# Moving the last pass over the tokens beside the last nine expert blocks of a two-layer kernel

## The chip, the core and the metric

The kernel runs on one core of a Trainium2 chip. The metric is the device time of one execution in microseconds; lower is better. All tensors are float32.

## What is computed

Two layers run over 4096 tokens (`B*S`) of 256 features. Each layer normalises `x`, computes a sequence-mixing term `s` and a mixture-of-experts term, and adds `s * silu(experts)` to `x`. The change touches only the end of layer 1 and a few things that it needs earlier:

```python
xn = _layernorm(x)
s = _L1_attn_ref(xn, ...)     # spectra of three projections, unit magnitude, product, cumsum over tokens, inverse
# mixture of 8 experts, two for every token
gate_scores = softmax(xn @ Wg + bg)
topk_scores, topk_idx = top_k(gate_scores, 2)
topk_scores = topk_scores / (sum(topk_scores) + 1e-08)
for e in range(8):
    h = gelu(xn @ W1[e] + b1[e])              # 256 -> 1024
    y = h @ W2[e] + b2[e]                     # 1024 -> 256
    output = output + y * combine_w[..., e:e + 1]
x = x + s * silu(output)
```

## The kernel before

**Order.** Everything is placed by hand. `schedule0` writes the plan of layer 0, `schedule1` that of layer 1: a list of items such as `("w1", n)`. Each engine walks the same list and carries out those items that concern it, in that order, so the list sets the order on every engine and on the DMA queues of SP (SyncE) and POOL (GpSimd). An item that waits holds everything behind it on its engine.

**Layer 1, attention.** The 4096 tokens are 16 chunks of 256. For a chunk, TensorE makes the spectra, ScalarE squares them (`squares`, L1963), POOL adds real and imaginary squares (L2074), ScalarE takes the root (`magnitudes`, L1970), which needs another activation table than GELU does (`ACT_TABLE_LOAD`), and VectorE does the rest of the chunk (`bind`, some 16 instructions). The spectra of the first eight chunks are made before the expert blocks; chunks 0 to 2 get their roots there too.

**Layer 1, routing.** Each token has two results, one for each of its two experts. Rows are sorted by expert into 71 tiles of 128 rows. VectorE finds which token stands in which row by comparisons (`rows_of`, 8 groups of `hot_tile`, L1626, and `hot_row`, L1629, multiplied by TensorE at L1143). Its answer is `token_of` (which row to fetch) and `result_of` (where the result goes, 0 to 8191).

**Layer 1, experts.** The tiles make 39 blocks: 32 pair blocks of two tiles (numbers 0 to 31) and then 7 single blocks of one tile. Block `n` runs as: POOL fetches its rows by an indirect DMA per tile (`xg`, L2086); TensorE turns them (L1165) and multiplies by `W1` (L1179) in eight pieces through three banks; ScalarE applies GELU to each piece (L1996); TensorE multiplies by `W2` (L1189); VectorE adds the bias (L1734); POOL scatters each tile into `result1` by an indirect DMA (L2097). SP loads each block's weights (L2239, 2180 KB) three blocks ahead. Chunk `n + 1` of the attention stands beside block `n`.

**The end.** When all results are in DRAM, item `last` goes over the tokens in eight quarters `q` of 512 tokens: SP loads both results of a quarter (`both`, L2251, 1 MB), ScalarE weighs the first (L2006), VectorE adds the weighed second (L1742), ScalarE applies SiLU (L2015), VectorE multiplies by `s` (L1753) and adds `x` (L1755), SP stores (L2254). `x` and `s` of all quarters (`xs`) were loaded at block 19 by one item (16 DMAs of 512 KB).

```python
# L2013: ScalarE, one quarter of the last pass
first = both[q][:, 0, :, :]
w.wait_ge(mixed1, q + 1)
e.activation(first, first, ACT.Silu).then_inc(gated1, 1)
```

## Time and profile before

| | us |
|---|---|
| median of 3 runs | 1188.36 (1184.89 to 1188.45) |
| the profiled execution's own time | 1180.72 |
| its span, first to last instruction | 1178.6 |
| PE busy | 1035.9 (88%) |
| DVE busy | 650.8 (55%) |
| ACT busy | 526.5 (45%) |
| POOL busy | 368.0 (31%) |

PE is TensorE's matrix products, PEld its weight loads, DVE VectorE, ACT ScalarE, POOL GpSimd, SP SyncE. An execution's own time is 2.1 us longer than its span. Busy shares are means over the whole span; what a piece of work costs has to be read in the stage where it stands. The page's busy line of PE by slices of 29.5 us reads 9 (90% or more) nearly everywhere from 118 us on, is lower around 420 to 560 us, and falls to 4 and then 0 in the last two slices.

### The profile page before, as it was taken

How to read it: one execution, taken by the hardware profiler on the slowest of the kernel's cores; microseconds unless marked ns; L12 is line 12 of the kernel's file. 1: busy time of each engine (PE TensorE's matmuls, PEld its weight loads, DVE VectorE, ACT ScalarE, POOL GpSimd, SP SyncE). 2: the span in 40 equal slices, each digit the busy share in tenths (PEclk: the TensorE clock that was granted, in tenths of full speed). 3: DMA queues.
4: the chain of work that ended last, by engine and by line, in shares of the span. 5: the costliest groups of instructions: out<-in, count | busy, mean ns of one | idle time of the engine just before them, and what ended most of it. 6: DMA issues, size and time to landing. Idle time of an engine off the chain costs nothing.

```text
span 1178.6 us, 16522 instructions
## 1 busy us (share of the span) xinstructions
PE 1035.9 (88%) x6152; PEld 889.6 (75%) x6152; DVE 650.8 (55%) x1379; ACT 526.5 (45%) x1079; POOL 368.0 (31%) x352
## 2 busy tenths in 40 slices
PE   4468999999999947887999999999999999999940
PEld 3347788888888835676878888888888888889930
DVE  7578776776777758686998566575300000000028
ACT  4324655554554456614354544454233323333445
POOL 1046545445445420003244232323222222222200
PEclk9779999999999988878999999999999999999975
DMA  9914234433444354344376334253555975555848
GB/s 299 266 55 145 80 107 123 145 105 111 131 131 120 121 181 161 118 191 163 122 267 250 137 139 170 108 198 134 193 203 198 360 303 195 204 201 192 328 144 283
DMA packets 100911, 208.65 MB, mean 177 GB/s; under 512 B 9850, under 2 KB 86150, under 8 KB 95840
## 3 DMA queue, kind: packets, MB, share of 16 engines
q1 hardware_dynamic: 89264, 176.27, 43.1%
q0 software_dynamic: 11568, 31.34, 8.0%
q8 instruction: 49, 0.80, 0.3%
q14 instruction: 30, 0.25, 0.1%
HBM read 159.86 MB, written 49.75 MB: 178 GB/s over the span
## 4 chain that ended last, share of the span: by engine, by line
PE 70%; DVE 15%; DMA 5%; ACT 4%; SPq 3%; issue 2%; POOL 0%; POOLq 0%; DVEq 0%; ACTq 0%
PE PS L1189 18%; PE PS L1179 17%; PE PS L1078 6%; PE PS L913 6%; PE PS L963 4%; PE PS L1017 3%; PE PS L972 2%; PE PS L1044 2%; PE PS L1088 2%; PE PS L1030 2%; PE PS L1055 2%; DVE hot_tile L1626 1%; SPq L2213 1%; SPq L2214 1%; DVE stats L1211 1%
## 5 line engine op out<-in xcount | busy, mean ns | idle before, releaser
L1996 ACT ACTIVATE hT<-PS,WE 128x256 f32<-128x256 f32 (+1 forms) x312 | 140.5, 455 | 281.6 <-PE PS L1179 278.2
L1179 PE MATMUL PS<-xgT,WE 128*128 128x256 f32 (+1 forms) x1248 | 256.2, 363 | 6.4 <-ACT hT L1996 4.1
L1189 PE MATMUL PS<-WE,hT 128*128 128x256 f32 x1136 | 251.6, 379 | 0.0
L1179 PEld LDWEIGHTS PS<-xgT,WE 128*128 128x128 f32 x1248 | 219.8, 191 | 35.9 <-ACT hT L1996 6.9
L1189 PEld LDWEIGHTS PS<-WE,hT 128*128 128x128 f32 x1136 | 213.4, 190 | 27.7
L1734 DVE TENSOR_TENSOR y<-PS,WE 128x512 f32<-128x512 f32 (+1 forms) x39 | 25.1, 643 | 353.0 <-PE PS L1189 353.0
L2097 POOL DMA_INDIRECT result<-y,result_of x71 | 71.7, 1009 | 285.0 <-DVE y L1734 271.2
L2074 POOL TENSOR_TENSOR MAG<-SQ 128x768 f32<-128x768 f32 x16 | 29.6, 1851 | 220.6 <-ACT SQ L1963 220.6
L913 PE MATMUL PS<-XT,Wf 128*128 128x256 f32 x384 | 96.1, 409 | 0.0
L913 PEld LDWEIGHTS PS<-XT,Wf 128*128 128x128 f32 x384 | 78.0, 208 | 11.4
L2086 POOL DMA_INDIRECT xg<-xn_dram,token_of x71 | 73.0, 1029 | 29.9 <-issue 21.5
L2055 POOL TENSOR_TENSOR prob<-prob,row_sum 128x512 f32<-128x512 f32 x56 | 58.6, 1047 | 59.9 <-DVE row_sum L1384 59.5
L1078 PE MATMUL PS<-rowsT,wgu 128*128 128x160 f32 x512 | 75.6, 301 | 0.0
L1078 PEld LDWEIGHTS PS<-rowsT,wgu 128*128 128x128 f32 x512 | 71.9, 190 | 2.3 <-issue 1.4
L2048 POOL TENSOR_TENSOR sc<-sc,sc_max 128x512 f32<-128x512 f32 x56 | 58.6, 1047 | 42.4 <-DVE sc_max L1372 42.1
L963 PE MATMUL PS<-XT,qkv_w 128*128 128x256 f32 x256 | 67.1, 409 | 0.0
L902 PE MATMUL PS<-const,XN 128*128 128x128 f32 x128 | 25.4, 331 | 45.4 <-DVE XN L1227 40.8
L1382 DVE TENSOR_REDUCE row_sum<-prob 128x8 f32<-128x512 f32 x64 | 43.6, 681 | 26.6 <-ACT prob L1864 25.8
L902 PEld LDWEIGHTS PS<-const,XN 128*128 128x128 f32 x128 | 17.2, 163 | 54.4 <-DVE XN L1227 23.3
L963 PEld LDWEIGHTS PS<-XT,qkv_w 128*128 128x128 f32 x256 | 49.7, 205 | 8.5 <-issue 0.4
L2066 POOL DMA_INDIRECT mixed_dram<-y,row_token x40 | 39.8, 996 | 47.3 <-DVE y L1438 42.9
L2039 POOL DMA_INDIRECT table<-XN,slot_put x32 | 32.0, 1001 | 66.3 <-DVE slot_put L1315 49.6
(240 smaller groups left out, 1600.8 us busy)
## 6 DMA issues: line engine op xcount, KB each, us to landing
WE<-in_experts SPq DMA_DIRECT2D x39, 2180.0 KB, 9.0
wgu<-in_w_gate SPq DMA_DIRECT2D x32, 256.0 KB, 2.8
wgu<-in_w_up SPq DMA_DIRECT2D x32, 256.0 KB, 3.2
wdn<-in_w_down SPq DMA_DIRECT2D x32, 256.0 KB, 3.5
both<-result SPq DMA_DIRECT2D x16, 512.0 KB, 8.8
table<-zeros POOLq DMA_DIRECT2D x1, 5160.0 KB, 32.7
rows<-table SPq DMA_DIRECT2D x32, 129.0 KB
X<-in_x SPq DMA_DIRECT2D x8, 512.0 KB, 8.7
```

The lines of the kernel that those rows point to most:

```text
L902: m = e.transpose(out_v[:, k, j * P:(j + 1) * P], XN[:, 2 * pair + j, k * P:(k + 1) * P], ident)
L913: m = e.matmul(PS[:, u.bank, part * CH:(part + 1) * CH], Wf[:, n, k, part * P:(part + 1) * P], XT1[:, ch, k, :], start=k == 0, stop=k == K ...
L963: m = e.matmul(PS[:, u.bank, c * UT:(c + 1) * UT], qkv_w[:, k, col:col + P], XT0[:, unit, k, :], start=k == 0, stop=k == KD - 1)
L1078: m = e.matmul(PS[:, u.bank + f, n * CAP:(n + 1) * CAP], wgu0[:, ex % 2, n, k, f * P:(f + 1) * P], rowsT[:, grp % 2, k, j * CAP:(j + 1) * ...
L1179: m = e.matmul(PS[:, FIRST_H_BANK + nth % HR, 0:rows], W1[n % WR][:, k, c * P:(c + 1) * P], xgT[:, n % 2, k, 0:rows], start=k == 0, stop=k ...
L1189: m = e.matmul(PS[:, u.bank, j * D:(j + 1) * D], hT[:, n % 2, c, j * P:(j + 1) * P], W2[n % WR][:, c, :], start=c == 0, stop=c == KF - 1)
L1382: e.tensor_reduce(row_sum[:, s % RR, :], prob[:, s % PR0, :, :], AX.X, ALU.add).then_inc(row_sum_done, 1)
L1996: e.activation(hT[:, n % 2, c, 0:rows], PS[:, FIRST_H_BANK + (KF * n + c) % HR, 0:rows], ACT.Gelu_apprx_tanh, bias=b1[n % WR][:, c:c + 1], ...
L2048: e.tensor_tensor(by_head, by_head, sc_max[:, s % SR, :].unsqueeze(2).to_broadcast([P, PAIRS, WIN]), ALU.subtract).then_inc(sc_sub_done, 1)
L2055: e.tensor_tensor(prob[:, s % PR0, :, :], prob[:, s % PR0, :, :], row_sum[:, s % RR, :].unsqueeze(2).to_broadcast([P, PAIRS, WIN]), ALU.mu ...
L2086: e.indirect_dma_start(out=xg[:, n % XR, j, :], out_offset=None, in_=xn_dram, in_offset=bass.IndirectOffsetOnAxis(ap=token_of[:, tile:tile ...
L2097: e.indirect_dma_start(out=result1, out_offset=bass.IndirectOffsetOnAxis(ap=result_of[:, tile:tile + 1], axis=0), in_=y1[:, n % YR, j, :], ...
```

## The change

The last pass is taken apart and put beside the last nine blocks, and the blocks are put in another order for it.

- **Blocks.** The single blocks stand among the pair blocks (positions 16, 18, ... 28), so that the last nine blocks (`EARLY` = 30 to `LAST` = 38) are pairs.
- **Two result tables.** The results of blocks 0 to 29 are scattered twice, into `result1` and `other1`; those of blocks 30 to 37 into `other1` alone; those of block 38 nowhere. Both tables are filled with zeros beforehand, by 32 DMAs of 512 KB in layer 0.
- **Quarters beside the blocks.** Item `last`'s eight quarters run in blocks 31 to 36 (1, 1, 1, 1, 2, 2 quarters). They read `result1`; a token with a result in a late block gets a value there that is overwritten later. SiLU is written as a tanh, which needs no other table than GELU: `0.5 z (1 + tanh(z/2))`.
- **Late rows.** For each of the 18 late tiles, POOL fetches `x`, `s` and the two weights of its tokens (`late_rows`, 2064-byte rows of a new table `late_dram`), and the token's other result from `other1` (`late_other`); VectorE and ScalarE finish those rows (`late_sum`, `late_gate`, `late_rest`), and POOL scatters them to the output after all quarters are stored (`late_put`). Where both results of a token are late, only the later row is put (`put_of`).
- **Last block.** Its `W2` product is made in two halves (`w2_last`), each finished by itself.
- **Root sums.** VectorE adds the squares of chunks 0 to 2 (`first_sum`) in place of POOL. The roots of chunks 3 and 4 stand at block 2 instead of block 1.
- **Small.** `xg` is fetched three blocks ahead instead of two; `xs` has five buffers, filled one a block from block 17; the weights are saved as 16-byte pieces in `late_dram` (4096 of them).

```diff
-SLOT_TILES = [2] * PAIR_SLOTS + [1] * SINGLE_SLOTS
+LATE, FIRST_SINGLE = 9, 16
+BLOCKS = [(2, 2 * n) for n in range(PAIR_SLOTS)]
+for n in range(SINGLE_SLOTS):
+    BLOCKS.insert(FIRST_SINGLE + 2 * n, (1, 2 * PAIR_SLOTS + n))
...
+XSR, BR, OR = 5, 3, 3
+XS_AT, LATE_ROWS_AT = CHUNKS + 1, CHUNKS + 1
+MIXED_AT = [[], [0], [1], [2], [3], [4, 5], [6, 7]]
+LAGGED = EARLY + len(MIXED_AT) - 1
+PUT_FIRST, PUT_SECOND = 4, 6
...
         if i == 4:
-            for ch in range(ROOTS_AHEAD):
-                add("squares", ch)
-    for ch in range(ROOTS_AHEAD):
-        add("magnitudes", ch)
+            for ch in range(2):
+                add("first_sum", ch)
+            add("squares", 2)
+            for ch in range(2):
+                add("magnitudes", ch)
+    add("first_sum", 2)
+    add("magnitudes", 2)
...
+        if n == 2:
+            add("magnitudes", ch)
+            add("magnitudes", ch + 1)
...
+        mixed = MIXED_AT[n - EARLY] if EARLY <= n <= LAGGED else ()
+        if EARLY + 2 <= n <= LAGGED + 1:
+            add("late_gate", n - 2)
+            add("late_rest", n - 2)
+        if n > LAGGED:
+            add("late_sum", n - 1)
+            add("late_gate", n - 1)
+            add("late_rest", n - 1)
+        for q in mixed:
+            add("weigh", q)
+            add("mix", q)
+        for q in mixed:
+            add("gate1", q)
+        if n < LAST:
+            add("w2", n)
+        else:
+            for j in range(2):
+                add("w2_last", j)
+        for q in mixed:
+            add("store", q)
+        if EARLY < n <= LAGGED:
+            add("late_sum", n - 1)
...
+        if n == LAST - 1:
+            for m in range(PUT_FIRST, PUT_SECOND):
+                add("late_put", EARLY + m)
+        if EARLY <= n + 1 < NSLOT:
+            add("late_other", n + 1)
+        if n == LAST - 2:
+            for m in range(PUT_FIRST):
+                add("late_put", EARLY + m)
+        if n == LAST - 1:
+            for m in range(EARLY + PUT_SECOND, LAST):
+                add("late_put", m)
...
+        def late_rest(n, some):
...
+            e.scalar_tensor_tensor(out=z, in0=gate, scalar=1.0, in1=z, op0=ALU.add, op1=ALU.mult).then_inc(
...
+            e.scalar_tensor_tensor(out=z, in0=z, scalar=0.5, in1=fin[:, tiles, D:2 * D], op0=ALU.mult, op1=ALU.mult).then_inc(
...
+            m = e.tensor_tensor(fin[:, tiles, 0:D], fin[:, tiles, 0:D], z, ALU.add)
...
+        def late_put(n, j):
+            tile = 2 * (n - EARLY) + j
+            w.wait_ge(late_ready, tile + 1 if n == LAST else tile - j + 2)
+            wait_stored(w, QUARTERS)
+            w.wait_ge(selected, 2)
+            e.indirect_dma_start(
+                out=out, out_offset=bass.IndirectOffsetOnAxis(ap=put_of[:, tile:tile + 1], axis=0), in_=fin[:, tile, 0:D],
...
+            elif what == "late_other":
+                wait_results1(w, n)
...
+            elif what == "store":
+                q, = at
+                w.wait_ge(out_ready, q + 1)
+                e.dma_start(out_view[:, 4 * q:4 * q + 4, :], xs[q % XSR][:, 0, :, :]).then_inc(stored[q % XSR], 16)
+                if q + BR < QUARTERS:
+                    load_both(q + BR)
+                if q and q - 1 + XSR < QUARTERS:
+                    load_xs(q - 1 + XSR)
```

On POOL, at the end of the program, these rows stood before (`result` is the scatter of a tile, `xg` the fetch):

```order
L2097 DMA result<-y_163,result_of 8192x256
L2086 DMA xg<-xn_dram,token_of 128x256
L2097 DMA result<-y_163,result_of 8192x256
L2086 DMA xg<-xn_dram,token_of 128x256
L2097 DMA result<-y_163,result_of 8192x256 x3
L2258 UNCONDITIONAL_BRANCH
```

and these stand there now, from block 35 on (`other<-y` is the scatter of a block's results, `other_174<-other` and its like the fetch of the other results for the next block, `out<-fin` the late rows to the output):

```order
L2328 DMA other<-y_176,result_of 8192x256 x2
L2351 DMA other_174<-other,other_of 128x256 x2
L2328 DMA other<-y_176,result_of 8192x256 x2
L2351 DMA other_178<-other,other_of 128x256 x2
L2294 DMA out<-fin,put_of 4096x256 x8
L2328 DMA other<-y_176,result_of 8192x256 x2
L2294 DMA out<-fin,put_of 4096x256 x4
L2351 DMA other_188<-other,other_of 128x256 x2
L2294 DMA out<-fin,put_of 4096x256 x6
```

Eight output scatters (those of blocks 30 to 33) stand between block 36's fetch and block 37's scatter, and four more (blocks 34 and 35) ahead of block 38's fetch.

On ACT, in the first expert blocks, stood before (`SQ` the squares of a chunk, `MAG` the roots, `hT` the eight GELUs of a block, from block 0 on):

```order
L1996 ACTIVATE hT<-PS,WE 128x256 x8
L1983 ACTIVATE xgT<-PS 128x512
L1963 ACTIVATE SQ<-Z 128x512 x3
L1996 ACTIVATE hT<-PS,WE 128x256 x8
L1983 ACTIVATE xgT<-PS 128x512
L1963 ACTIVATE SQ<-Z 128x512 x3
L1970 ACT_TABLE_LOAD
L1970 ACTIVATE MAG<-MAG 128x768 x2
L1996 ACT_TABLE_LOAD
L1996 ACTIVATE hT<-PS,WE 128x256 x8
```

and now:

```order
L2215 ACTIVATE hT<-PS,WE 128x256 x8
L2202 ACTIVATE xgT<-PS 128x512
L2182 ACTIVATE SQ<-Z 128x512 x3
L2215 ACTIVATE hT<-PS,WE 128x256 x8
L2202 ACTIVATE xgT<-PS 128x512
L2182 ACTIVATE SQ<-Z 128x512 x3
L2215 ACTIVATE hT<-PS,WE 128x256 x8
L2202 ACTIVATE xgT<-PS 128x512
L2189 ACT_TABLE_LOAD
L2189 ACTIVATE MAG<-MAG 128x768 x2
L2182 ACTIVATE SQ<-Z 128x512 x3
L2215 ACT_TABLE_LOAD
```

The pair of table loads has moved from ahead of block 2's GELUs to behind them, ahead of a chunk's squares.

On DVE, in the last groups of the routing, stood before:

```order
L1626 TENSOR_SCALAR hot_tile<-const,tile_f 128x71 x8
L1629 TENSOR_TENSOR hot_row<-const,in_tile 128x1024
L1636 COPY row_v<-PS 128x71
L1638 TENSOR_SCALAR row_empty<-row_v 128x71
L1639 TENSOR_SCALAR row_v<-row_v 128x71
```

and now, from group 4 on:

```order
L1772 TENSOR_SCALAR hot_tile<-const,tile_f 128x71 x8
L1775 TENSOR_TENSOR hot_row<-const,in_tile 128x1024
L1782 TENSOR_TENSOR MAG<-SQ 128x768 x2
L1772 TENSOR_SCALAR hot_tile<-const,tile_f 128x71 x8
L1775 TENSOR_TENSOR hot_row<-const,in_tile 128x1024
L1772 TENSOR_SCALAR hot_tile<-const,tile_f 128x71 x8
L1775 TENSOR_TENSOR hot_row<-const,in_tile 128x1024
L1772 TENSOR_SCALAR hot_tile<-const,tile_f 128x71 x8
L1775 TENSOR_TENSOR hot_row<-const,in_tile 128x1024
L1782 TENSOR_TENSOR MAG<-SQ 128x768
L1786 COPY row_v<-PS 128x71
```

The three sums (`MAG<-SQ`) have come to DVE, two behind group 4 and one behind group 7; POOL has none of them any more.

## Rows read from the trace of the kernel before

**Rows 1.** Stages: length, busy (count) of PE, PEld, DVE, ACT, POOL; clock, DMA, GB/s

```profile
500.00:560.00 60.00, 47.49 (x236) 42.47 (x236) 46.16 (x142) 20.52 (x40) 11.48 (x9) 0.77 0.46 180
...
860.00:920.00 60.00, 60.00 (x288) 52.83 (x287) 2.77 (x4) 17.41 (x36) 16.25 (x16) 1.00 0.55 205
920.00:960.00 40.00, 38.32 (x184) 33.46 (x183) 2.08 (x3) 12.86 (x27) 12.19 (x12) 1.00 1.06 385
```

**Rows 2.** Waits of PE over 560 to 1132 us: total, times, longest us

```profile
PE PS L1179 <- ACT hT L1996: 4.1, 7, 2.9
PE PS L1179 <- DMA WE<-in_experts: 1.7, 1, 1.7
PE PS L1165 <- DMA xg<-xn_dram,token_of: 0.7, 1, 0.7
```

**Rows 3.** Timeline of the end: start us, us, instructions [idle before <-releaser]

```profile
1128.28 3.62 PE L1189 MATMUL PS<-WE,hT 128*128 128x256 f32 x16
...
1131.93 0.42 DVE L1734 TENSOR_TENSOR y<-PS,WE 128x256 f32<-128x256 f32 x1 [6.60 <-PE PS L1189]
1133.13 0.97 POOL L2097 DMA_INDIRECT result<-y,result_of  x1 [6.05 <-DVE y L1734]
...
1140.82 1.71 ACT L2006 ACTIVATE both<-both,weight 128x256 f32<-128x256 f32 x4 [10.46 <-DMA both<-result]
...
1145.44 1.04 ACT L2015 ACTIVATE both<-both 128x1024 f32<-128x1024 f32 x1
...
1168.80 1.66 DVE L1742 SCALAR_TENSOR_TENSOR both<-both,weight 128x256 f32<-128x256 f32 x4
...
1174.03 1.22 DVE L1755 TENSOR_TENSOR xs<-xs,both 128x1024 f32<-128x1024 f32 x1
```

**Rows 4.** Chain that ended last, the result's scatter: start us, us, what

```profile
1133.13 2.08 DMA result<-y,result_of
```

**Rows 5.** Timeline of POOL in a stretch of plain pair blocks

```profile
866.32 1.01 POOL L2097 DMA_INDIRECT result<-y,result_of  x1 [10.17 <-DVE y L1734]
867.64 0.99 POOL L2097 DMA_INDIRECT result<-y,result_of  x1 [0.30 <-issue]
...
880.59 1.01 POOL L2097 DMA_INDIRECT result<-y,result_of  x1 [9.30 <-DVE y L1734]
```

**Rows 6.** Groups over 860 to 920 us: count, busy us, mean ns

```profile
L1996 ACT ACTIVATE hT<-PS,WE 128x256 f32<-128x256 f32 x32 | 15.2, 474 | 39.6 <-PE PS L1179 39.6
...
L1734 DVE TENSOR_TENSOR y<-PS,WE 128x512 f32<-128x512 f32 x4 | 2.8, 692 | 53.4 <-PE PS L1189 53.4
...
L1983 ACT ACTIVATE xgT<-PS 128x512 f32<-128x512 f32 x4 | 2.4, 597 | 0.0
```

**Rows 7.** DMA issues of the page: count, KB each, median us to landing

```profile
WE<-in_experts SPq DMA_DIRECT2D x39, 2180.0 KB, 9.0
...
both<-result SPq DMA_DIRECT2D x16, 512.0 KB, 8.8
...
out<-xs SPq DMA_DIRECT2D x8, 512.0 KB, 4.9
```

**Rows 8.** Timeline of the routing's last groups

```profile
531.92 1.90 DVE L1626 TENSOR_SCALAR hot_tile<-const,tile_f 128x71 f32<-128x71 f32 x8 [2.78 <-PE PS L1143]
...
537.81 6.53 DVE L1626 TENSOR_SCALAR hot_tile<-const,tile_f 128x71 f32<-128x71 f32 x8
537.96 5.42 POOL L2074 TENSOR_TENSOR MAG<-SQ 128x768 f32<-128x768 f32 x3 [113.64 <-ACT SQ L1963]
```

**Rows 9.** Timeline of expert blocks 1 and 2

```profile
590.19 1.28 ACT L1970 ACT_TABLE_LOAD   x1
...
591.48 1.58 ACT L1970 ACTIVATE MAG<-MAG 128x768 f32<-128x768 f32 x2
...
608.55 0.69 DVE L1734 TENSOR_TENSOR y<-PS,WE 128x512 f32<-128x512 f32 x1 [0.77 <-PE PS L1189]
...
610.34 1.21 POOL L2097 DMA_INDIRECT result<-y,result_of  x1 [3.97 <-issue]
```

More of the change, by code:

```diff
@@ L27 @@
 PAIR_SLOTS, SINGLE_SLOTS = T * TOPK // (2 * P), E1 - 1
[L28 to L29 removed]
+LATE, FIRST_SINGLE = 9, 16
+BLOCKS = [(2, 2 * n) for n in range(PAIR_SLOTS)]
+for n in range(SINGLE_SLOTS):
+    BLOCKS.insert(FIRST_SINGLE + 2 * n, (1, 2 * PAIR_SLOTS + n))
+SLOT_TILES, SLOT_AT = [tiles for tiles, _ in BLOCKS], [at for _, at in BLOCKS]
 NSLOT = len(SLOT_TILES)
+EARLY, LAST = NSLOT - LATE, NSLOT - 1
+LATE_AT, LATE_TILES = SLOT_AT[EARLY], 2 * LATE
+assert all(BLOCKS[EARLY + n] == (2, LATE_AT + 2 * n) for n in range(LATE))
 TILES1 = sum(SLOT_TILES)
@@ L473, in add @@
             banks.take(item, 5)
+        elif what == "w2_last":
+            banks.take(item, (5, 7)[at[0]])
     def spectra(ch):
@@ L499, in schedule1 @@
             add("owners")
+        if i == 1:
+            add("squares", 0)
+            add("squares", 1)
         if i in (2, 4):
@@ L864, in wait_attn1_end @@
         w.wait_ge(summed, 2 * CHUNKS)
-    def wait_experts_read(w):
-        for n in (NSLOT - 2, NSLOT - 1):
-            u = use["w2", n]
-            w.wait_ge(full[u.bank], u.filled)
     def score_of(PS, s):
@@ L1190, in tensor @@
                                      W2[n % WR][:, c, :], start=c == 0, stop=c == KF - 1)
+                m.then_inc(full[u.bank], 1)
+            elif what == "w2_last":
+                j, = at
+                u = use["w2_last", j]
+                fill_from(u)
+                for c in range(KF):
+                    w.wait_ge(gelu_done, KF * LAST + c + 1)
+                    m = e.matmul(PS[:, u.bank, 0:D], hT[:, LAST % 2, c, j * P:(j + 1) * P], W2[LAST % WR][:, c, :],
+                                 start=c == 0, stop=c == KF - 1)
                 m.then_inc(full[u.bank], 1)
@@ L1632, in vector @@
                                 ALU.is_equal).then_inc(hot_row_ready, 1)
+            elif what == "first_sum":
+                ch, = at
+                w.wait_ge(squared, ch + 1)
+                e.tensor_tensor(MAG[:, ch, :, :], SQ[:, ch % 2, :, 0, :], SQ[:, ch % 2, :, 1, :], ALU.add).then_inc(mag_ready, 1)
             elif what == "rows_found":
@@ L1732, in vector @@
                 else:
[L1733 removed]
+                    w.wait_ge(y_out[n % YR], y1_landed(n % YR, n))
                 e.tensor_tensor(y1[:, n % YR, 0:tiles, :], PS[:, u.bank, 0:tiles * D].rearrange("p (j d) -> p j d", d=D),
                                 b2[n % WR].unsqueeze(1).to_broadcast([P, tiles, D]), ALU.add).then_inc(free[u.bank], 1)
[L1736 to L1755 removed]
@@ L2126, in load_gate_up, with zero_results @@
                 e.dma_start(wgu0[:, ex % 2, n, :, :], a[name][ex].rearrange("(k p) n -> p k n", p=P)).then_inc(gu_in[ex % 2], 16)
+        def zero_results(ex):
+            nth = ZERO_AT.index(ex)
+            first = ZERO_ROWS * nth
+            w.wait_ge(filled, 4)
+            for results in (result1, other1):
+                e.dma_start(results[first:first + ZERO_ROWS, :].rearrange("(r p) d -> p r d", p=P),
+                            zeros[:, 0:D].unsqueeze(1).to_broadcast([P, ZERO_ROWS // P, D])).then_inc(results_zeroed, 16)
         def load_down(ex):
```

381 lines of the change are left out of this document (279 added, 102 removed).

## The prediction, written before the changed kernel ran

> **What bounds the kernel now.** I read the stages first: from the end of the routing on, TensorE has no gap to speak of. In a stretch of plain pair blocks it is busy for 60.00 of 60 us at the full clock, while VectorE has 2.77 us of work, ScalarE 17.41 and POOL 16.25 [rows 1]. The waits of TensorE over the whole of the blocks come next: 4.1 us for GELU (one of 2.9), 1.7 for weights, 0.7 for rows [rows 2]. So work of the other engines is free beside the blocks as long as nothing waits for it, and TensorE's time there can hardly shrink. Third, the timeline of the end: TensorE's last product ends at 1128.28 + 3.62 = 1131.9, the span at 1178.6. For 46.7 us TensorE has nothing to do: bias and scatter (landed at 1135.2), a load, and eight quarters at some 4.1 us of VectorE each (1.66 and twice 1.22), its last addition starting at 1174.03 [rows 3, 4]. Last, the stretch of 500 to 560 us, where TensorE works 47.49 of 60 us at a granted 0.77 and waits for VectorE's routing [rows 1, 8].
>
> **The end, new.** The eight quarters go beside blocks 31 to 36. A pair block's period is 880.59 - 866.32 = 14.27 us [rows 5]. I follow the last blocks from t = 0, the end of block 35's products.
>
> VectorE first: bias 0.7 [rows 6], then three operations of 1024 columns for each of quarters 4 and 5. The trace has no scalar_tensor_tensor of that width; four of 256 took 1.66, a tensor_tensor of 1024 took 1.22 [rows 3]; I take 1.22, the row of the same width. That is 3.7 a quarter, ending at 8.1. Block 34's sums (four operations of 256 columns, 0.42 each) end at 9.8. ScalarE has by then finished block 36's GELUs and the copy (7.5 + 0.6, at 8.1 [rows 6]); tanh of block 34 to 10.7, weighing of quarters 6 and 7 (1.71 each [rows 3]) to 14.1. VectorE does the rest of block 34 (three of 512 columns at 0.69 [rows 6]) to 12.8 and the two mixes (1.66 each) to 16.2; ScalarE's last tanh (1.04 [rows 3]) ends at 17.2. Block 37's GELUs stand behind it. TensorE starts block 37 at 14.27, fills three banks (of eight pieces in half a period, 0.9 each) in 2.7 and wants the first GELU's answer by 17.0; it comes at 17.2 + 0.47: a stall of 0.7 us. The single-quarter blocks have room.
>
> VectorE's bias of block 36 ends at 16.9, its six operations at 24.2; the last quarter is stored 4.9 later [rows 7], at 29.1. Only then do POOL's output scatters start. One indirect DMA takes POOL 1.32 from start to start [rows 5]. Eight of them: 39.7. Block 37's two scatters, which have been ready since about 31: 42.3. Four more output scatters: 47.6. The two fetches for block 38: the second starts at 48.9 and, with 2.08 from start to landing in a quiet stretch [rows 4], lands at 51.0. TensorE ends at 14.27 + 0.7 + 14.27 + 13.8 = 43.0 (the last block turns no rows for a next one, an estimate of 0.5 less). So VectorE's last work waits for the queue, not for TensorE. From 51.0: scaling two tiles 0.8; for each half bias 0.42, sum 0.41, tanh 0.43, three operations of 0.42 and some 0.2 of hand-overs, 2.7; twice is 5.4, at 57.2; from there to the landing of the last scatter 1135.2 - 1132.35 = 2.9 [rows 3, 4], at 60.1. The tail is 17.1 us in place of 46.7: **-29.6**, and **+0.7** for the stall.
>
> **Other terms.** (a) In the routing's last group, eight comparisons that take 1.90 take 6.53 beside POOL's three sums of 5.42 [rows 8]. They go to VectorE: 768 columns, between 0.69 and 1.22 each, two of them in the 2.78 us in which VectorE waits for TensorE behind group 4 [rows 8], one behind group 7, while TensorE multiplies that group. So 4.6 us go; two small copies of the changed `owners` add 0.3: **-4.3**. (b) TensorE's wait of 2.9 in block 2 goes with the table loads ahead of its GELUs [rows 2, 9]. They now stand where TensorE has block 2's second product, 7 us, against 6.5 of ScalarE: a copy of 0.6, two loads of 1.28, two roots of 1.58 together, three squares of 512 columns at the copy's 0.6 [rows 6, 9]. VectorE gets chunk 3's roots some 4 us later; in block 2 its bias waited only 0.77 for TensorE [rows 9], but block 3's second product comes 8 us behind it and is what needs it: **-2.9**, at worst 0. (c) The wait of 1.7 for weights stands where 16 loads of 512 KB go out at once, at 385 GB/s [rows 1, 2]; they are now spread: **-1.7**. The 0.7 for rows in the single blocks goes too: there is one single block in 21.5 us and three blocks of advance: **-0.7**. (d) The zeros are 32 x 0.5 MB in layer 0, where I found no load that TensorE waits for, the 4096 pieces of 16 bytes stand ahead of the spectra's saves, and blocks 0 to 29 scatter 53 tiles twice. POOL has 53 x 1.32 = 70 us more in some 440, and it idles for 10 us in each plain block [rows 5]; nothing waits for the second copies. No row prices the 16-byte pieces; they can't gain anything, and the nearest row, 512 KB of output in 4.9 [rows 7], is my upper bound; I take **+1.5** for all of (d).
>
> Sum: -29.6 + 0.7 - 4.3 - 2.9 - 1.7 - 0.7 + 1.5 = -37.0. Against the profiled execution's own 1180.7 that is 1143.7. The runs shown have a median of 1188.4, 7.6 above it; the difference belongs to both kernels alike, so 1151.4, and I forecast **1151**. A change of under 0.3% (3.6 us) can't be told from none.
>
> **Rivals.**
>
> *The queue doesn't hold the end.* If stores land sooner and block 38's rows are fetched before TensorE is done, the tail is one half's 2.7 and the landing of 2.9, 5.6: 11.5 better, 1140. It needs block 38's fetch some 12 us sooner: a store that lands as fast as the scatter's 2.08 in place of 4.9 [rows 4, 7], less work of VectorE than I count, or scatters closer together than 1.32. For it, the DMAs are quiet by then; against it, VectorE has some 15 us of work in a block with two quarters, so that quarter 7 can't come much sooner. 12%.
>
> *Crowded transfers, and ScalarE in order.* A late block moves 2.2 MB of weights, 1.05 of results in, 0.52 of output, 0.79 of rows and, three times, 1.05 of `x` and `s`: 5.6 MB in 14.27 us is 395 GB/s, above the 385 of the busiest stretch, in which TensorE did wait [rows 1]. Each quarter's weighing stands ahead of a block's GELUs; where its load comes late, TensorE stops. Against it: loads are issued two blocks before use, except quarter 7's (one block, some 6 us of spare against 8.8 to landing [rows 7]). With 2.5 us in each of six blocks: +15, 1166. 19%. By the Trainium skill (DMA: Bandwidth & Descriptors, Specifications) HBM gives a core about 358 GB/s; the 385 of the trace is above that, one core running alone here. At 358 the three blocks would fall behind by 1.5 us each, an estimate that would make this rival likelier.
>
> *POOL slowed by VectorE.* Beside a busy VectorE one scatter took 1.21 instead of 1.01 [rows 5, 9]. With 0.2 more on each of the 16 operations between the last store and block 38's fetch: +3.2, 1155. 9%. The Trainium skill (DMA: Bandwidth & Descriptors, SWDGE vs HWDGE vs iDMA) says why it may be so: POOL writes its descriptors to on-chip memory that VectorE's two-port modes lock it out of. The trace agrees by those 0.2 us.
>
> *The gains ahead don't come.* If chunk 3's later roots or the pieces of 16 bytes give back (a) and (b): +7, 1158. 9%.
>
> *Slower.* SP's queue becomes the clock: a block's weight load now stands behind the store of a quarter, which waits for VectorE, which waits for ScalarE, which waits for a load that itself stands behind weights. If that ring closes, each of blocks 31 to 38 lasts longer than 14.27; from 4.6 us a block on (37 / 8) the change loses. At 6 us a block it would be 1151 + 48 = 1199. Against it: three weight buffers give two blocks, 28 us, against 9.0 to landing [rows 7]. 4%. Something between this and the crowded case, within 0.3% of before: 2%.
>
> **Numbers.** The forecast has 45% with 1145 to 1157, the rivals 12, 19, 9, 9, 4 and 2. For 8 in 10 I take in the first and most of the crowded case: 1139 to 1167. Faster 0.94, same 0.02, slower 0.04.
>
> **What would show it.** Right: TensorE's last product some 15 to 18 us ahead of the end; POOL back to back with output scatters, and a wait of VectorE's for a fetch of `other` in that tail; `hot_tile` without a 6.5 us group; no wait over 1 us for GELU in block 2; blocks 30 to 38 at 14.3 us. Wrong: periods above 15 us there (crowding: TensorE waiting for `hT` behind `both`), a tail of under 8 (the queue), or a stretch of 500 to 560 us in which TensorE is no busier than 47.49.

## The result, and the profile after

The first set of runs gives 1192.10 us as the median of 7 for the changed kernel against 1187.19 for the kernel before, in the same set: a ratio of 1.0048, 95% interval 1.0025 to 1.0072. That is a loss of half a per cent, small but outside the noise. I had forecast 1151 us, and the time lies outside my range. The profiled execution took 1186.6 us, its span is 1184.8.

The same kernel was then run again, on other chips, as the baseline of the experiments. The comparison comes out in two ways, and each whole set lies on one side:

| set | chip | before, median (n) | changed, median (n) | ratio (95%) |
|---|---|---|---|---|
| 1 | not known | 1187.19 (7) | 1192.10 (7) | 1.0048 (1.0025 to 1.0072) |
| 3 | index 0 | 1180.38 (11) | 1157.91 (4) | 0.9803 (0.9771 to 0.9836) |
| 4 | index 8 | 1179.19 (11) | 1156.61 (7) | 0.9814 (0.9796 to 0.9831) |
| 5 | index 13 | 1180.34 (7) | 1159.57 (4) | 0.9840 (0.9796 to 0.9885) |
| 6 | index 14 | 1186.19 (25) | 1190.56 (10) | 1.0047 (1.0018 to 1.0076) |

Sets 2 (chip index 9, before 1178.26) and 7 (index 0 again, before 1185.02) held other kernels. I call 1, 6 and 7 the late sets, for what their traces show, and 2 to 5 the clear sets. The trace of before shown ahead of the prediction is a clear one: its 1180.72 us lie under all seven timed runs of its own set (1182.30 to 1188.45), and only 12 of its 8480 DMA semaphore updates are missing (a clear trace of the changed kernel lacks none to 14 of 10,688).

First the stages of the late trace, in the stretches of [rows 1] (length, busy time of PE, PEld, DVE, ACT, POOL, then clock, DMA share, GB/s), with 960 to 1030 added:

```profile
500.00:560.00 60.00, 51.15 (x250) 45.44 (x248) 47.89 (x157) 22.38 (x45) 6.07 (x6) 0.80 0.49 162
860.00:920.00 60.00, 54.95 (x273) 46.67 (x271) 2.66 (x5) 17.11 (x41) 27.08 (x28) 0.94 0.79 287
920.00:960.00 40.00, 34.04 (x176) 28.76 (x177) 1.81 (x3) 10.80 (x27) 15.44 (x16) 1.00 0.81 303
960.00:1030.00 70.00, 64.22 (x341) 55.25 (x340) 6.03 (x33) 22.30 (x53) 38.19 (x38) 1.00 0.73 269
```

From the trace of the same kernel in set 4:

```profile
860.00:920.00 60.00, 60.00 (x333) 54.23 (x333) 3.35 (x6) 21.04 (x50) 32.38 (x33) 1.00 0.91 341
920.00:960.00 40.00, 40.00 (x224) 36.14 (x223) 2.23 (x4) 13.37 (x34) 21.45 (x22) 1.00 0.84 313
960.00:1030.00 70.00, 70.00 (x352) 62.14 (x351) 13.17 (x44) 26.68 (x58) 36.84 (x37) 1.00 0.80 287
```

TensorE loses 16.8 of 170 us in the late trace, by its busy time, and nothing in the clear one, whose DMA moves more in the same time. The stalls cost clock as well. After a stretch in which TensorE worked 2.21 of 5 us the granted clock falls to 0.50, its lower level of 1.2 GHz, from 894.1 to 900.9 us:

```profile
890.00:895.00 5.00, 2.21 (x8) 1.31 (x8) 0.00 (x0) 0.47 (x1) 3.72 (x4) 0.91 1.12 416
895.00:900.00 5.00, 4.41 (x11) 3.52 (x12) 0.00 (x0) 2.38 (x6) 0.00 (x0) 0.50 0.94 384
```

TensorE is busy for 5.3 us of that, so I estimate 2.7 us lost to the clock. PE's waits from 560 us on, late (set 1) and then clear (set 4):

```profile
PE PS L1281 <- issue: 13.6, 13, 2.4
PE PS L1281 <- ACT hT L2215: 9.3, 14, 3.4
PE PS L1267 <- DMA xg<-xn_dram,token_of: 2.5, 1, 2.5
```

```profile
PE PS L1281 <- ACT hT L2215: 7.7, 8, 3.4
```

L1281 is the `W1` product. "issue" means that the view knows no releaser; the timeline of pair block 19 in the late trace shows one (start us, us, instructions, idle before and releaser):

```profile
885.02 2.75 PE L1281 MATMUL PS<-xgT,WE 128*128 128x256 f32 x12
887.05 1.00 POOL L2315 DMA_INDIRECT xg<-xn_dram,token_of  x1 [0.30 <-issue]
888.03 0.47 ACT L2215 ACTIVATE hT<-PS,WE 128x256 f32<-128x256 f32 x1 [5.33 <-PE PS L1281]
888.56 1.13 PE L1281 MATMUL PS<-xgT,WE 128*128 128x256 f32 x4 [0.79 <-issue]
891.53 0.47 ACT L2215 ACTIVATE hT<-PS,WE 128x256 f32<-128x256 f32 x1 [1.63 <-PE PS L1281]
892.06 1.13 PE L1281 MATMUL PS<-xgT,WE 128*128 128x256 f32 x4 [0.98 <-issue]
893.62 1.01 POOL L2315 DMA_INDIRECT xg<-xn_dram,token_of  x1 [0.31 <-issue]
895.07 0.47 ACT L2215 ACTIVATE hT<-PS,WE 128x256 f32<-128x256 f32 x1 [3.06 <-remote]
895.59 3.78 PE L1281 MATMUL PS<-xgT,WE 128*128 128x256 f32 x8 [2.40 <-issue]
```

TensorE runs three pieces through its three banks and stops; ScalarE stands idle and starts the first GELUs 2 to 5.4 us after their pieces ended (a piece ends by 886.0, its GELU starts at 888.03; the fourth piece, of 888.56 to 889.69, gets its GELU at 895.07); 0.05 us behind each GELU TensorE goes on. So neither engine is slow and no data are missing; I read this as TensorE's completion signals arriving late, and TensorE's own DRAIN in the later traces (below) bears it out. They cost time in the pair blocks 19, 21, 23, 25 and 29, each behind a single block, while POOL issues 12 indirect DMAs in a row (13 in the last one). Here the row is from 879.2 to 894.6 us, and the signals are on time from 895.1 on. The length of the row does not decide alone: block 27 has a row of 11 over 14.1 us beside its product, GELUs there are 1.6 us late at most, and TensorE loses nothing; and in this trace the row of 20 at the end (1145.9 to 1172.8 us) delays none of TensorE's signals that the trace shows. What is different there is not known. In the clear trace the same row stands beside the same product:

```profile
893.55 7.07 PE L1281 MATMUL PS<-xgT,WE 128*128 128x256 f32 x32
894.69 0.47 ACT L2215 ACTIVATE hT<-PS,WE 128x256 f32<-128x256 f32 x1 [3.81 <-PE PS L1281]
895.47 0.47 ACT L2215 ACTIVATE hT<-PS,WE 128x256 f32<-128x256 f32 x1 [0.31 <-PE PS L1281]
895.62 1.00 POOL L2315 DMA_INDIRECT xg<-xn_dram,token_of  x1 [0.30 <-issue]
```

The page of the late trace has a second mark: DMAs without a landing time. Late, then clear:

```profile
WE<-in_experts SPq DMA_DIRECT2D x39, 2180.0 KB
```

```profile
WE<-in_experts SPq DMA_DIRECT2D x39, 2180.0 KB, 10.3
```

Each DMA gives 16 semaphore updates, 10,688 in this kernel. The late traces record 7991 (set 1) and 7884 (set 6) of them, the clear ones at least 10,674. The Trainium skill (NOTIFIC — the notification-queue block, Overflow: three behaviours, one of which stalls the engine) says that a full notification queue either loses records or stalls the engine that makes them. Lost records and late signals stand together in all five late traces (one in set 1, three in set 6, one in set 7). That does not make the queue the cause: no run here shows the queue itself, the losses are also where nothing is late (34 to 36 updates of 128 in each of blocks 6 to 12 of the first late trace), and a run of set 5 loses some without a late signal. The timed runs are late as well.

The end, in the late trace (DVE and POOL rows chosen; TensorE's last product ends at 1161.06):

```profile
1153.99 7.07 PE L1300 MATMUL PS<-WE,hT 128*128 128x256 f32 x32
1163.80 0.98 POOL L2294 DMA_INDIRECT out<-fin,put_of  x1 [0.30 <-issue]
1166.43 1.02 POOL L2351 DMA_INDIRECT other<-other,other_of  x1 [0.30 <-issue]
1169.37 0.80 DVE L1601 TENSOR_SCALAR other<-other,other_weight 128x256 f32<-128x256 f32 x2 [11.86 <-DMA other<-other,other_of]
1175.10 0.42 DVE L1615 TENSOR_TENSOR fin<-fin,other 128x256 f32<-128x256 f32 x1
1176.32 0.97 POOL L2294 DMA_INDIRECT out<-fin,put_of  x1 [1.71 <-DVE fin L1615]
```

The tail is 1184.8 - 1161.1 = 23.7 us in place of 46.7 [rows 3]; in the clear traces it is 23.8, 21.7 and 29.2. VectorE waits for the fetch behind POOL's puts, as forecast. Behind the last put's landing stands POOL's own last instruction, a DRAIN, from 1178.81 to 1184.60 us. In the trace of before POOL's DRAIN is at 1132.91, 5.36 us long, and nobody waits for it.

In the four late traces of sets 6 and 7 the tail has late signals too, and longer ones. In `combined` (set 6) TensorE's last product ends at 1144.80, the other results are scaled by 1149.22, and VectorE gets to the last block's bias at 1156.65, 2.4 us behind POOL's row:

```profile
1142.70 2.10 PE L1297 MATMUL PS<-WE,hT 128*128 128x256 f32 x9
1153.24 0.98 POOL L2291 DMA_INDIRECT out<-fin,put_of  x1 [0.30 <-issue]
1156.65 0.42 DVE L1939 TENSOR_TENSOR y<-PS,WE 128x256 f32<-128x256 f32 x1 [7.43 <-remote]
```

TensorE's own DRAIN ends 11.8 to 14.8 us behind its last product in these four, and within 0.1 us of it in the other traces. VectorE so waits 3.9 us in `after_fifth` and `end_on_sp`, 7.4 and 5.9 in `combined` and `combined_again`; no edit was aimed at this.

Routing in the clear trace of set 4 (DVE; the comparisons of the last groups, then the third root sum), which answers to [rows 8]:

```profile
528.22 1.90 DVE L1772 TENSOR_SCALAR hot_tile<-const,tile_f 128x71 f32<-128x71 f32 x8 [0.83 <-PE PS L1245]
534.12 1.89 DVE L1772 TENSOR_SCALAR hot_tile<-const,tile_f 128x71 f32<-128x71 f32 x8
537.06 0.95 DVE L1782 TENSOR_TENSOR MAG<-SQ 128x768 f32<-128x768 f32 x1
```

No group takes 6.53 us any more. And ScalarE ahead of block 4 in the same trace, which answers to [rows 9]:

```profile
613.88 1.67 ACT L2182 ACTIVATE SQ<-Z 128x512 f32<-128x512 f32 x3 [6.76 <-DMA Z<-z_dram]
615.57 1.28 ACT L2189 ACT_TABLE_LOAD   x1
616.86 1.58 ACT L2189 ACTIVATE MAG<-MAG 128x768 f32<-128x768 f32 x2
618.45 1.28 ACT L2215 ACT_TABLE_LOAD   x1
620.28 3.94 PE L1281 MATMUL PS<-xgT,WE 128*128 128x256 f32 x17 [3.40 <-ACT hT L2215]
```

### The profile page after: what moved, and what is told of

Its sections match the earlier page's. It is cut to its first block, busy times and chain, and to the rows that moved or that the text cites. A ratio compares the mean times of both kernels' runs of the same rounds, so it can differ in the third digit from the quotient of the medians.

```text
span 1184.8 us, 16922 instructions
## 1 busy us (share of the span) xinstructions
PE 1043.2 (88%) x6152; PEld 888.3 (75%) x6152; DVE 693.6 (59%) x1487; ACT 529.1 (45%) x1095; POOL 478.0 (40%) x454
## 4 chain that ended last, share of the span: by engine, by line
PE 69%; DVE 14%; ACT 5%; issue 5%; DMA 4%; POOL 1%; another core or an unknown queue 1%; SPq 1%; POOLq 0%; DVEq 0%; ACTq 0%
PE PS L1281 18%; PE PS L1291 18%; PE PS L1180 6%; PE PS L1015 5%; PE PS L1065 4%; PE PS L1119 3%; PE PS L1074 2%; PE PS L1190 2%; PE PS L1146 2%; PE PS L1132 2%; PE PS L1157 2%; PE PS L1267 1%; DVE stats L1322 1%; PE PS L1256 1%
## 5 line engine op out<-in xcount | busy, mean ns | idle before, releaser
L1281 PE MATMUL PS<-xgT,WE 128*128 128x256 f32 (+1 forms) x1248 | 265.1, 368 | 23.5 <-issue 13.6
L1281 PEld LDWEIGHTS PS<-xgT,WE 128*128 128x128 f32 x1248 | 220.3, 193 | 61.0 <-issue 19.1
L1291 PE MATMUL PS<-WE,hT 128*128 128x256 f32 x1104 | 245.2, 380 | 0.0
L1291 PEld LDWEIGHTS PS<-WE,hT 128*128 128x128 f32 x1104 | 208.0, 191 | 27.2
L2315 POOL DMA_INDIRECT xg<-xn_dram,token_of x71 | 78.6, 1107 | 144.9 <-DVE result_of L1800 121.1
L2328 POOL DMA_INDIRECT result<-y,result_of x53 | 53.4, 1007 | 159.7 <-DVE y L1884 150.3
L2328 POOL DMA_INDIRECT other<-y,result_of x69 | 70.0, 1014 | 28.0 <-issue 19.8
L1065 PE MATMUL PS<-XT,qkv_w 128*128 128x256 f32 x256 | 64.6, 398 | 0.0
L1479 DVE TENSOR_TENSOR sc<-PS,rel 128x512 f32<-128x512 f32 x64 | 43.2, 675 | 20.8 <-remote 7.5
```

The costliest lines, as they stand in the source:

```text
L1065: m = e.matmul(PS[:, u.bank, c * UT:(c + 1) * UT], qkv_w[:, k, col:col + P], XT0[:, unit, k, :], start=k == 0, stop=k == KD - 1)
L1281: m = e.matmul(PS[:, FIRST_H_BANK + nth % HR, 0:rows], W1[n % WR][:, k, c * P:(c + 1) * P], xgT[:, n % 2, k, 0:rows], start=k == 0, stop=k ...
L1291: m = e.matmul(PS[:, u.bank, j * D:(j + 1) * D], hT[:, n % 2, c, j * P:(j + 1) * P], W2[n % WR][:, c, :], start=c == 0, stop=c == KF - 1)
L1479: e.tensor_tensor(by_half(sc[:, r, :, :, :]), score_of(PS, s), by_half(rel[:, :, :, :]), ALU.add).then_inc(free[u.bank], 1)
L2315: e.indirect_dma_start(out=xg[:, n % XR, j, :], out_offset=None, in_=xn_dram, in_offset=bass.IndirectOffsetOnAxis(ap=token_of[:, tile:tile ...
L2328: e.indirect_dma_start(out=results, out_offset=bass.IndirectOffsetOnAxis(ap=result_of[:, tile:tile + 1], axis=0), in_=y1[:, n % YR, j, :], ...
```

## The experiments

Periods are those of the `W1` products' starts. Without stalls the interleaved blocks 16 to 30 take 7.5 (from a single to the next pair) and 14.0 us in turn.

**Set 2: is it POOL's row of DMAs, the bytes, or the order?**

`one_table`, results of blocks 0 to 29 into one table (the late rows then lack their other results, which the edit leaves out):

```diff
-                    for results in (result1, other1) if n < EARLY else (other1,):
+                    for results in (result1,) if n < EARLY else (other1,):
```

> Results of blocks 0 to 29 go into one table only (the second table then lacks them, so the late rows use zeros there: that part is left out). In the changed kernel PE loses 25 us between block 16 and block 38 against 14.25 us a pair and 7.25 us a single; the loss stands inside the W1 products of pair blocks 19, 21, 23, 25 and 29, while POOL issues 12 indirect DMAs in a row (15.4 us). Theory A (the loss comes when a long row of POOL's indirect DMAs meets full DMA queues): bursts fall from 12 to 9, their last 4 us go, about half of the 25 us goes, time near 1180. Rival B (bytes alone: 2180 KB of weights for every single block, and xs): only 0.26 MB of some 5 MB per 21.5 us goes, so under 3 us, time 1189 to 1193. Rival C (the order of blocks alone, a single before a pair): nothing, 1192.

1153.26 us, 0.9787 of before (0.9759 to 0.9815); no stall in blocks 16 to 30.

`rows_by_sp`, the late rows by plain loads (of other rows, and each output scatter waits for the one before it, so only the blocks ahead of the end are read):

```diff
-                e.indirect_dma_start(out=fin[:, i, :], ..., in_=late_dram, ...)      # POOL
+                e.dma_start(fin[:, i, :], late_view[:, i, :]).then_inc(late_rows_in, 16)   # SP
```

> The 18 late_rows gathers of POOL become plain loads of as many bytes by SP (of other rows, so the late rows' values are left out), and each put waits for the one before it, which lengthens the end only: to be read from PE's times between block 16 and block 38, not from the time. Theory A (number of POOL's indirect DMAs in a row): bursts of 9, about half of the 25 us goes. Rival B (bytes): the same bytes, the 25 us stay.

One execution, 1185.25 us: 7.5 and 14.0 us a block, no stall.

`one_and_sp`, both edits:

> Both edits together (one table, late rows by SP, puts in order): bursts of 6 as in the late blocks 31 to 33, which lose nothing. Theory A: under 3 us of the 25 us left between block 16 and block 38. Rival B (bytes): over 20 us left. To be read from PE's times, as the end is lengthened.

One execution, 1183.08 us. The same: 7.5 and 14.0 us, no stall.

`singles_together`:

```diff
-    BLOCKS.insert(FIRST_SINGLE + 2 * n, (1, 2 * PAIR_SLOTS + n))
+    BLOCKS.insert(FIRST_SINGLE + n, (1, 2 * PAIR_SLOTS + n))
```

> The changed kernel with its seven single blocks at positions 16 to 22 in a row instead of 16, 18, ... 28; nothing left out. Theory A (a row of 12 indirect DMAs of POOL beside full DMA queues): a pair then issues 8 in a row and a single 4, so the 25 us of stalls go in blocks 23 to 29; in the singles weights of 2180 KB and 1 MB of xs per 7.25 us may cost up to 10 us; time 1168 to 1180. Rival B (bytes alone): the same bytes in less time while the singles run, the loss moves there and stays 25 us or more, 1190 to 1200. Rival C (a pair after a single stalls): one such place left, 1170.

1162.37 us, 0.9854 (0.9827 to 0.9882). No stall inside products; 7.7 us lost at blocks 20 to 22, where the wait view names the weights: `PE PS L1281 <- DMA WE<-in_experts: 5.1, 3, 2.8`. So this order makes a loss at the loads that the unedited one doesn't have on a clear chip.

All four went theory A's way, two of them further than it said (the whole loss gone, not half), and they proved nothing: set 2 had no run of the unedited kernel.

**Set 3: the unedited kernel beside its edits.**

`after_again`, the changed kernel as it is:

> The changed kernel once more, on one chip with the three others and the kernel before. If its loss belongs to the kernel, pair blocks 19 to 29 again show W1 products of 10 to 14 us and the ratio to before is again 1.000 to 1.010; if it was that one execution, the intervals from block 16 to 30 are 14.0 and 7.5 us and the ratio is 0.98.

1157.91 us, 0.9803 (0.9771 to 0.9836). No stall. The first set's loss is not the kernel's alone, and set 2 says nothing on it.

`broken_burst`, a wait that parts POOL's row:

```diff
             elif what == "late_rows":
-                i, = at
+                i, n = at
                 wait_attn1_end(w)
+                if SLOT_TILES[n] == 1:
+                    w.wait_ge(gelu_done, KF * (n + 2))
```

> The changed kernel with one wait more: the late_rows gather of a single block waits until the next block's W1 product has passed GELU, so POOL's 12 indirect DMAs of 21.5 us stand as 9 and 3 instead of in one row; number, bytes and order are the same, nothing is left out. Theory A (too many of POOL's indirect DMAs in a row or in flight at once): no stall in W1 products, 14.0 and 7.5 us a block, 25 us less, ratio to before 0.975 to 0.985. Rival D (the number of indirect DMAs in 21.5 us, or how many semaphore updates they bring, wherever they stand): 12 are still there, the stalls stay, ratio 0.995 or more.

1158.28 us, 0.9823 (0.9796 to 0.9850): no different from the unedited kernel, as it can't be where there is nothing to mend. Its trace shows the row parted as 10 and 2, not 9 and 3.

`best`, the same with two edits at the end:

```diff
-MIXED_AT = [[], [0], [1], [2], [3], [4, 5], [6, 7]]
-PUT_FIRST, PUT_SECOND = 4, 6
+MIXED_AT = [[], [0], [1], [2], [3, 4], [5, 6], [7]]
+PUT_FIRST, PUT_SECOND = 4, 5
```

> broken_burst and two more edits: the quarters of the last pass stand as 1, 1, 1, 2, 2, 1 in blocks 31 to 36 instead of 1, 1, 1, 1, 2, 2, so that in block 37 GELU does not stand behind two quarters that wait for their loads (that cost 1.7 to 4.8 us between blocks 37 and 38), and four of the six puts ahead of block 38's fetch on POOL's queue become two (2.6 us earlier fetch). Expected 4 to 7 us below broken_burst, ratio to before 0.970 to 0.978; if POOL's put row alone sets the end, the first edit gives nothing and it is 2 to 3 us.

1153.54 us, 0.9789 (0.9761 to 0.9817). Its tail is 19.4 us where `broken_burst` has 23.0, 3.6 us less in one pair of executions; the tails of the unedited kernel alone differ by 7.5 us from trace to trace, and set 4 has 21.1 against 21.7, so what the earlier fetch is worth isn't settled. The stall of 2 us only moves from block 37 to block 36.

`four_tables`, an edit of the kernel before:

```diff
+                    for results in (result1, *more) if n >= 16 else (result1,):
```

> The kernel BEFORE, with the results of blocks 16 to 38 scattered into three more tables that nobody reads: a pair block then has 10 indirect DMAs of POOL in a row (12.8 of 14.25 us) instead of 4, beside the same weight loads. Theory A: W1 products of pair blocks 17 to 31 stall as in the changed kernel, by 3 to 8 us a block in several of them, 15 us or more in all. Rival E (it needs the changed kernel's extra loads by SP in the same microseconds): 14.25 us a block as before, and only the last landing later.

One execution, 1203.53 us. Ten in a row give no late signal here, but nor do twelve in this set (`after_again`), so this says nothing on a late chip. What they give is late data: PE waited 9.3 us for rows (one wait of 8.6) and 7.6 for weights between 840 and 1150 us. On this clear chip the longer rows cost landings.

**Set 4: again, with a trace of before.**

> The changed kernel a third time, as it is. It measured 1.0048 times the kernel before with stalls inside the W1 products of blocks 19 to 29 (25 us), and then 0.9803 with none of them. If the stalls are drawn anew in each execution, some of these executions lie near 1185 to 1195 and some near 1158. If they belong to where or on which chip the kernel runs, all of them lie on one side, as in both sets so far: ratio 0.978 to 0.984 where there are no stalls, 1.000 to 1.008 where there are.

1156.61 us, 0.9814 (0.9796 to 0.9831), all seven runs between 1150.30 and 1158.92: whole sets, not executions, lie on one side.

> The kernel before once more, for a trace of it from the same chip as the changed kernel's. If the first set of runs was on a slower chip or placement, before too is some 7 us faster now (1178 to 1181 in place of 1187), and the 7 us stand where its DMAs or semaphores are late (layer 0 until 430 us, the start of the blocks, the loads of xs at blocks 22 and 23); if it is the same chip and state, its stages stand as in the first trace within 1 us.

One execution, 1178.47 us, span 1176.4. Its stages are those of the first trace of before but for 2.4 us ahead of the first block. That one was a clear trace, so before was never traced in a late set, and where its 7 us go there is open.

> The version with the broken burst, the quarters 1, 1, 1, 2, 2, 1 and two puts ahead of the last fetch, beside the changed kernel on the same chip: 4 to 5 us below it where the changed kernel has no stalls (0.996 of it), 25 to 30 us below it where it has, if the row of 12 indirect DMAs is what the stalls need.

1154.67 us, 0.9792 (0.9767 to 0.9818) beside 0.9814: better by less than the intervals.

**Set 5.**

> The changed kernel once more. If the stalls belong to a chip or placement and this one is like the last two: 0.979 to 0.983 of before, 7.5 and 14.0 us a block from 16 to 29, no missing semaphore updates. If this is one like the first: 1.000 to 1.008, before at 1185 or more, stalls and missing updates together.

1159.57 us, 0.9840 (0.9796 to 0.9885), 10,676 of 10,688 updates.

`many_updates`, behind each weight load from block 19 on:

```diff
+                    for i in range(12):
+                        e.dma_start(tiny_dram[n, i, :, :], a["const"][0:16, 0:16]).then_inc(wf_in, 16)
```

> The changed kernel with 12 tiny loads by SP (16 rows of 64 bytes, 16 semaphore updates each) behind the weights of every block from 19 on, queued beside the rest; nothing is left out. Semaphore updates of DMAs rise from about 12 to about 25 a microsecond in blocks 16 to 35, bytes by nothing. Theory F (late signals come from too many semaphore updates in a short time): GELU starts 1 us and more behind the end of a W1 piece in pair blocks, updates are missing from the trace, 10 us or more lost between block 16 and block 30. Rival G (they come from something of the chip or placement of the first set, not from the number): no late GELU, no missing updates, at most some 5 us lost to SP's longer queue.

One execution, 1161.91 us. The trace has 2930 semaphore updates of all kinds in the 100 us from 900 on, where `after_fourth` has 1441, and no GELU starts late. The number of updates alone doesn't do it. Of the 14,528 updates of DMAs that this kernel makes, 275 are missing from the trace: some records can be lost without a late signal. The longer SP queue cost 1.4 us at block 25 and 9.4 at block 37.

`roots_back`:

```diff
-        if n == 2:
-            add("magnitudes", ch)
-            add("magnitudes", ch + 1)
-        if n % 2 and n > 1:
+        if n % 2:
```

> The changed kernel with one edit undone: the roots of chunks 3 and 4 stand in block 1 again, as in the kernel before, and not in block 2. My prediction gave the move 2.9 us of gain; PE's time from block 0 to block 16 was 291.5 before and 290.4 to 293.7 after. If the move only carries the stall from block 2 (GELU 4.1 us late) to block 4 (4.7 us late, because the next chunk's squares there wait for their spectra), this kernel has its stall at block 2 again, 290 to 293 us from block 0 to 16, and the same total within 2 us. If the move was worth its 2.9 us and something else took them, this kernel is 3 us slower.

1155.33 us, 0.9796 (0.9764 to 0.9827). GELU starts 3.6 us late at block 2 in place of 4.7 (set 4) at block 4; block 0 to 16 takes 292.3 us. The move was worth nothing; whether it cost the difference to `after_fourth` the intervals don't tell.

**Set 6: a late chip.**

> The changed kernel, as baseline on the chip of the two others: 0.979 to 0.984 of before, or 1.000 to 1.008 with late signals and missing updates if this is a chip like the first.

1190.56 us, 1.0047 (1.0018 to 1.0076). Late signals and missing updates are back together, in the same blocks. The first set is reproduced.

`end_on_sp`:

```diff
                     late_put(LAST, j)
-                w.wait_ge(late_stored, 16 * LATE_TILES)    # POOL
...
                 wait_stored(w, QUARTERS)
+                w.wait_ge(late_stored, 16 * LATE_TILES)    # SP
```

> The changed kernel with one line moved: SP, not POOL, waits at the end for the last put to land. Theory H (POOL's DRAIN takes its 5.8 us wherever it begins and does not wait for the DMA): it begins 1.3 us behind the last put's start in place of 2.5 us, the span behind the last put's start falls from 8.5 us to about 7.0 us, 1.3 to 1.5 us less in all, which the medians hardly show and the trace does. Rival I (the DRAIN is the wait for outstanding DMAs): its end stays 8.3 us behind the last put's start and nothing is gained. Rival J (the DRAIN is short where POOL has not just waited): 4 us or more gained.

1188.03 us, 1.0011 (0.9987 to 1.0034). From the last put's start to the end it is 7.0 us; with the wait on POOL it is 8.5. The DRAIN begins with the put and takes 7.0 us; it had begun 2.5 us behind the put's start and taken 5.8. So the sum is that of theory H, and its reason isn't: the DRAIN's length is not fixed. It is 8.1 us in `rows_by_sp` and 3.8 in `one_and_sp`, and what sets it is open. The medians, 1190.56 and 1188.03, can't tell the 1.5 us.

`combined`, all edits: `best`, `roots_back`, `end_on_sp`.

> All edits together: broken burst, quarters 1, 1, 1, 2, 2, 1, two puts ahead of the last fetch, roots of chunks 3 and 4 in block 1, the end wait on SP. Sum of what was measured apart: puts 3 us, end 1.4 us, roots 0 to 3 us, the others nothing where there are no late signals: 4 to 7 us below the changed kernel, ratio to before 0.974 to 0.979.

1177.42 us, 0.9940 (0.9914 to 0.9966): 13 us under the unedited kernel on the same chip. The two traced executions are 20.3 us apart in span (1169.9 and 1190.2), and 13.0 of these stand in blocks 16 to 30: they take 17.8 us more than the clear traces' 150.7, where `after_fifth` takes 30.8 more. Parting POOL's row is the only edit that touches these blocks. A good part of the 13 is clock: in `after_fifth` it is granted at 0.50 for 17 us of these blocks, an estimated 7.9 us lost by TensorE's busy time there; in `combined` it never falls. PE's waits from 560 us on:

```profile
PE PS L1278 <- ACT hT L2212: 8.4, 14, 1.7
PE PS L1278 <- issue: 7.2, 8, 1.7
```

The part of POOL's row that is left still costs. In block 19 it ends here, 5.5 us of pause ahead of the next:

```profile
882.45 0.99 POOL L2325 DMA_INDIRECT other<-y,result_of  x1 [0.30 <-issue]
888.95 1.04 POOL L2337 DMA_INDIRECT fin<-late_dram,token_of  x1 [5.51 <-ACT hT L2212]
```

and GELU's last late start is this, 8.6 us behind the product's start (876.5), where the first late trace has 895.07, 10.1 us behind it:

```profile
885.12 1.20 ACT L2212 ACTIVATE hT<-PS,WE 128x256 f32<-128x256 f32 x3 [1.65 <-PE PS L1278]
885.65 1.99 PE L1278 MATMUL PS<-xgT,WE 128*128 128x256 f32 x8 [0.99 <-ACT hT L2212]
```

**Set 7.**

> The combined version as it is, on another chip. On one without late signals: blocks 16 to 30 at 7.5 and 14.0 us, the sum of its parts against the changed kernel's 0.980 to 0.984 (puts 3 us, roots 0 to 3, end wait 1.4): 1150 to 1153 us, ratio 0.974 to 0.978. On one like chip 14: 0.994 again, 3 to 4 us lost in each of blocks 19, 21, 23, 25 and 29.

1180.98 us, 0.9963 (0.9943 to 0.9984), before 1185.02: late again, 8093 of 10,688 updates recorded, though the chip's index is that of the clear set 3. The index alone is not the cause. On a clear chip the combined version wasn't run; the nearest that was, `best`, gave 0.9789 and 0.9792.

## Why the prediction was wrong

**The step that failed in the first set** is (d): "POOL has 53 x 1.32 = 70 us more in some 440, and it idles for 10 us in each plain block; nothing waits for the second copies". It is true that nothing waits for them, and on a clear chip blocks 16 to 30 lose nothing (`after_again`). But I counted POOL's load by its average. With singles between the pairs and late rows added, 11 to 13 of its DMAs stand in one row of 14 to 17 us beside a pair's `W1` product, and in the late sets TensorE's signals are late beside five of these six rows. Blocks 16 to 30 take 24.8 us more than in the clear traces (set 1), 30.8 and 27.3 (set 6). Blocks 31 to 36, with rows of 2 to 6, lose nothing, and with the row parted the loss is 17.8 and 15.2 us. That the row takes part is shown by these; that it is enough is not, for the row of 11 at block 27 costs 0 to 0.8 us in the same traces. The clock has a part of its own: an estimated 2.7, 7.9 and 3.1 us of the 24.8, 30.8 and 27.3, and none of the 17.8 and 15.2. None of my rivals was this one. "Crowded transfers" had the size (+15) but the wrong blocks: at 30 to 36, where I feared it, the period is 14.3 us, in the late traces too. Of the rest of the late sets' loss, TensorE's end of layer 0 comes 3 to 8 us later than in the clear traces of the same kernel (434.3 and 434.6 against 426.9 to 431.0 us), where POOL also issues eight in a row; what of that is the same cause wasn't tested.

The whole miss of the first set adds up in its trace. My sum makes a span of 1178.6 - 37.0 = 1141.6, and it is 1184.8. Some 11 us are ahead of block 16, which starts at 855.9 where my sum has 844.7; about 25 lie between there and TensorE's last product, 24.8 of them in blocks 16 to 30; 6.6 are in the tail.

**A sign I read past.** I put the profiled execution 7.6 us below its set and wrote that "the difference belongs to both kernels alike". It was the mark of two surroundings. By the medians before loses 5 to 9 us in a late set; the changed kernel loses 31 to 35.5.

**On a clear chip** the direction and the mechanism hold, but 21 to 23 us are gained, not 37. That the time, 1156.6 to 1159.6, lies in my range is in part luck: I had added the 7.6 us of a late set to a clear trace, and without them my figure would have been 1143.7. Term by term, from the traces of both kernels in set 4 (spans 1148.5 and 1176.4, a pair 5 us farther apart than the medians):

| term | predicted | measured |
|---|---|---|
| tail | -29.6 | -25.0 (46.7 to 21.7; 23.8 and 29.2 in the other two) |
| (a) routing, first to last comparison | -4.3 | -4.8 (34.0 to 29.2) |
| (b) roots at block 2 | -2.9 | -1.1 in set 4; about 0 over all: block 0 to 16 takes 291.5 before, 290.4 to 293.7 after |
| (c) loads of weights and rows | -2.4 | -3.1 by the periods |
| ScalarE's stall at block 37 | +0.7 | +5.0 (2.6 and 1.6 in the other two) |
| (d) end of routing to first rows turned | +1.5 | +2.2 (+4.7 and +3.5 in the other two) |

The measured terms add up to -26.8 of the -27.9.

*Tail.* The put row, the wait for the fetch and the end of VectorE's work are right: 14.2 us behind TensorE predicted, 14.5 measured in set 1 (12.4 to 19.9 in the clear traces). Missing is POOL's DRAIN of 5.8 us. In [rows 3, 4] the end is an SP store, and no row of them shows that a program whose last DMA is POOL's ends 6 us after it landed. *(b)* I took the stall of block 2 for the table loads' own. It belongs to three things in a line, and the first is the wait of 6.76 us for the next chunk's spectra from DRAM. That line stands ahead of whichever block comes; the move carried it to block 4. *Block 37.* I took its quarters' loads as landed; ScalarE waited 3.57 us for the first (`one_table`) and TensorE 2.4. *(d)* TensorE turns the first rows when block 0's second fetch has landed, 6.5 us after its start instead of 4.2. POOL issues six fetches in a row there in both kernels; new beside them are the 16-byte pieces (4253 packets under 512 B in 20 us, where before has 96). That these do it is argued, not tried.

What stays open is why a set is late. Late signals and a quarter of the updates missing come together in five traces and are absent in the fifteen others. The number of updates doesn't bring them about, nor does the chip's index. Missing records come without late signals too (`many_updates`, and blocks 6 to 12 of the late traces), so they are a mark of a late set; no run shows what makes the signals late.

## What to carry to other kernels

Work that goes to a queue "with idle time" is counted by the length of its longest row, not by its share: it is worth parting rows of POOL's indirect DMAs that stand beside a product whose pieces are handed to another engine through few banks (13 us here in a late set, nothing in a clear one). A stall there can also cost the clock, so what it is worth is read from the granted clock as well as from the waits. Run the unedited kernel in every set with its experiments; four results went my theory's way until it was there. Look at who has the last DMA in flight (moving the wait for it from POOL to SP gave 1.5 us in the trace, too little for the medians), and where a profiled execution lies outside its set's runs, ask which surroundings each belongs to before adding the difference.
